# Gathering relation products instead of node rows: a graph network kernel with tables of products, 128 edges a gather, 128 nodes a window

## What is computed

```python
def _rgcn_conv(x, src, dst, et, basis, comp, root, bias):
    W = jnp.einsum('rb,bio->rio', comp, basis)          # 8 matrices 128 x 128
    xw = jnp.einsum('ni,rio->nro', x, W)
    msgs = xw[src, et]
    seg = dst * N_REL + et
    summed = jax.ops.segment_sum(msgs, seg, num_segments=N_NODES * N_REL)
    cnt = jax.ops.segment_sum(jnp.ones((msgs.shape[0],), x.dtype), seg, num_segments=N_NODES * N_REL)
    mean = summed / jnp.maximum(cnt, 1.0)[:, None]
    agg = mean.reshape(N_NODES, N_REL, HIDDEN).sum(axis=1)
    return agg + x @ root + bias
...
for l in range(N_LAYERS):
    h_new = jax.nn.relu(_rgcn_conv(h, src, dst, edge_type, basis[l], comp[l], root[l], bias[l]))
    h = h_new + h
x = _layernorm(x + h, axis=-1)
```

## Time and profile before

| | |
|---|---|
| median of 3 runs | 5051.21 us |
| the profiled execution, its own time | 5047.87 us |
| its span, first to last instruction | 5046.1 us |
| granted TensorE clock, mean | 0.829 of full |
| busy: PE, ACT, DVE, POOL | 65%, 45%, 36%, 76% of the span |
| moved by DMA | 241.73 MB, 48 GB/s |

### The profile page before, as it was taken

The page is one execution under the profiler, slowest core; times in us unless marked ns, Lnnn a source line. Parts: engine busy times, 40 slices in busy tenths (PEclk is TensorE's granted clock), DMA queues, the critical chain, the costliest instruction groups (busy, mean ns, idle before and its releaser), DMA issues.

```text
span 5046.1 us, 91632 instructions
## 1 busy us (share of the span) xinstructions
PE 3255.1 (65%) x20895; PEld 3007.8 (60%) x20895; DVE 1839.1 (36%) x6662; ACT 2286.4 (45%) x6539; POOL 3838.0 (76%) x3447
## 2 busy tenths in 40 slices
PE   6277766666666666666676666666666666666667
PEld 4166665666555566655555656655665665656656
DVE  8444433333333333333333333333333333333335
ACT  4165544444444444444454444444444444444445
POOL 7877777777777777777767777777777777777775
PEclk9599988877888888888888887788778778887888
DMA  6111111111111111111121111111111111111114
GB/s 106 51 41 43 44 43 44 43 43 44 43 44 43 43 44 43 44 43 43 43 80 44 43 44 43 43 44 43 44 43 43 44 43 44 43 43 44 43 44 119
DMA packets 287032, 241.73 MB, mean 48 GB/s; under 512 B 164335, under 2 KB 238267, under 8 KB 286987
## 3 DMA queue, kind: packets, MB, share of 16 engines
q0 software_dynamic: 216448, 209.55, 16.7%
q10 hardware_dynamic: 32488, 15.69, 1.4%
q1 hardware_dynamic: 38051, 15.98, 1.2%
HBM read 224.50 MB, written 14.44 MB: 47 GB/s over the span
## 4 chain that ended last, share of the span: by engine, by line
POOL 55%; issue 42%; DMA 1%; DVE 1%; SPq 0%; PE 0%; ACT 0%; POOLq 0%; DVEq 0%; ACTq 0%
POOL ring L299 54%; POOL S L333 0%; DMA h_rows<-S 0%; DMA S<-counts,idxg 0%; SPq L366 0%; DMA ring<-x,idx 0%; DVE W L267 0%; ACT S L562 0%; PE bank L662 0%; DVE aggT L859 0%; PE bank L673 0%; POOL aggT L348 0%; DVE hT L890 0%; DMA onehot<-x 0%; DVE S L837 0%
## 5 line engine op out<-in xcount | busy, mean ns | idle before, releaser
L662 PE MATMUL bank<-onehot,rows 119*128 119x128 f32 x9856 | 1702.2, 328 | 1618.4 <-ACT rows L523 1456.4
L523 ACT ACTIVATE rows<-ring,relnorm 119x128 f32 x4928 | 1569.0, 389 | 2520.4 <-SPq L401 1755.2
L662 PEld LDWEIGHTS bank<-onehot,rows 119*128 119x128 f32 x9856 | 1476.1, 230 | 1811.1 <-issue 1040.4
L299 POOL DMA_INDIRECT ring<-x,idx x1600 | 1807.8, 1130 | 543.5 <-issue 526.6
L299 POOL DMA_INDIRECT ring<-h_rows,idx x1600 | 1762.5, 1102 | 537.4 <-issue 524.0
L849 DVE TENSOR_TENSOR onehot<-bank,relnorm 119x512 f32<-119x512 f32 x1232 | 851.4, 691 | 1764.5 <-issue 1266.3
L673 PE MATMUL bank<-S,W 128*128 128x128 f32 x9856 | 1488.4, 316 | 1.4 <-ACT S L505 1.4
L673 PEld LDWEIGHTS bank<-S,W 128*128 128x128 f32 x9856 | 1455.7, 234 | 1.8 <-ACT S L505 1.8
L859 DVE TENSOR_TENSOR aggT<-aggT,bank 128x16 f32 x4928 | 833.4, 169 | 1337.1 <-PE bank L673 843.1
L505 ACT ACTIVATE S<-bank 128x512 f32<-128x512 f32 x1232 | 708.0, 575 | 15.1 <-PE bank L662 14.8
L299 POOL DMA_INDIRECT ring<-h_rows,idx_rest x81 | 89.2, 1102 | 26.0 <-issue 26.0
(11 more groups left out here) (114 smaller groups left out, 587.2 us busy)
## 6 DMA issues: line engine op xcount, KB each, us to landing
ring<-x,idx POOLq DMA_INDIRECT x1600
ring<-h_rows,idx POOLq DMA_INDIRECT x1600
S<-x ACTq DMA_DIRECT2D x24, 256.0 KB, 4.0
h_rows<-S SPq DMA_DIRECT2D x24, 256.0 KB, 3.0
onehot<-x ACTq DMA_DIRECT2D x24, 256.0 KB, 3.4
out<-S SPq DMA_DIRECT2D x24, 256.0 KB, 3.2
idx<-srcT SPq DMA_DIRECT2D x64, 23.2 KB
ring<-x,idx_rest POOLq DMA_INDIRECT x81
```

The costliest lines, as they stand in the source:

```text
L299: g.indirect_dma_start(out=ring[0:R, slot * P:(slot + 1) * P], out_offset=None, in_=table, in_offset=bass.IndirectOffsetOnAxis(ap=index, a ...
L523: s.activation(rows[0:R, u % 2 * BATCH + k, :], ring[0:R, bass.ds(v[2 * k + 1], P)], ACT.Copy, scale=relnorm[0:R, 1, bass.ds(b * BATCH + k ...
L662: last = t.matmul(bank[2 * (u % 2) + k // 4][:, k % 4 * P:(k % 4 + 1) * P], rows[0:R, at, :], onehot[0:R, at, :], start=True, stop=True)
```

## The change

At the head of a layer every node is multiplied by all eight W, and the products are stored in a DRAM table of 100,000 rows of 128 numbers (row 8 n + r for node n and relation r), one table a layer. 98 tiles of up to 128 nodes are taken in turn: two matmuls 128 x 512 (`multiply`), two ACT copies into one of six stages of 4 KB per partition (`keep_products`; the stages lie in `ring`), one store of 512 KB from SP's queue (`store_products`). The first gather of the layer waits for all 98 stores. The gathers then fetch product rows by the index 8 src + relation, which DVE makes at the head and which goes through a DRAM tensor `idxT`.

A tile is 128 edges: 1563 tiles. A window is 128 nodes: 98 windows. The 0/1 matrix is 128 edges x 128 nodes and the scatter's result is the sum itself. `S`, its copies (L505) and `project` (L673) are gone. There are 1563 + 98 - 1 = 1660 steps in 208 batches. DVE adds 128 x 128 numbers a step, straight from the scatter's PSUM banks, one batch behind (AFTER = 1). `h1_rows` and its transposes, copies and stores are gone. Layer 0's W are made between the transposes of x, layer 1's after the products of layer 0. The root products follow the table.

```diff
-    R = 119
+    R = 128
...
-    WIN = P // RELS
+    WIN = P
...
-    h1_rows = nc.dram_tensor("h1_rows", (N, H), F32).ap()
+    products = [nc.dram_tensor(f"products{n}", (N * RELS, H), F32).ap() for n in range(LAYERS)]
+    idxT = nc.dram_tensor("idxT", (R, TILES), I32).ap()
...
+        stage = ring[:, 0:STAGES * RELS * H].rearrange("p (s c) -> p s c", s=STAGES)
...
+            pool.wait_ge(idx_made, 1)
+            g.dma_start(idxT, src_all).then_inc(idx_out, 16)
...
+            for L in layers:
+                for q in range(STAGES):
+                    pool.wait_ge(L.stored[q], 16 * stored_count(q))
+                turn(L, 0)
...
+            def store_products(L):
+                for i in range(NODE_TILES):
+                    w = tile_nodes_of(i)
+                    sp.wait_ge(L.staged, 2 * i + 2)
+                    sp.dma_start(products[L.n].rearrange("(n r) f -> n (r f)", r=RELS)[w, :],
+                                 stage[0:w.stop - w.start, i % STAGES, :]).then_inc(L.stored[i % STAGES], 16)
...
+            def keep_products(L):
+
+                for i in range(NODE_TILES):
+                    n = tile_nodes_of(i).stop - i * P
+                    if i >= STAGES:
+                        act.wait_ge(L.stored[i % STAGES], 16 * (i // STAGES))
+                    for half in range(2):
+                        j = 2 * i + half
+                        act.wait_ge(L.multiplied, j + 1)
+                        s.activation(stage[0:n, i % STAGES, half * 512:(half + 1) * 512],
+                                     bank[T_BANKS[L.n][j % len(T_BANKS[L.n])]][0:n, :], ACT.Copy).then_inc(L.staged, 1)
...
-                    if k % 4 == 3 and (not isinstance(b, int) or b >= 1) and not is_last(b):
-                        keep_half(L, b - 1, (u + UNROLL - 1) % UNROLL, k // 4)
...
+            def multiply(L, i):
+
+                w, banks = tile_nodes_of(i), T_BANKS[L.n]
+                for half in range(2):
+                    j = 2 * i + half
+                    if j >= len(banks):
+                        pe.wait_ge(L.staged, j - len(banks) + 1)
+                    t.matmul(bank[banks[j % len(banks)]][0:w.stop - w.start, :], hT[:, w],
+                             W[:, L.n, half * 512:(half + 1) * 512], start=True, stop=True).then_inc(L.multiplied, 1)
...
-            def project(L, b, u, lots):
-
-                pe.wait_ge(L.s_kept, 2 * b + 2)
...
+                if not isinstance(b, int) or b >= PB:
+                    pe.wait_ge(L.added, (b - PB + 1) * BATCH)
...
-                if k == 0:
-                    dve.wait_ge(L.projected, b + 1)
+                if k % 4 == 0:
+                    dve.wait_ge(L.scattered, 2 * b + k // 4 + 1)
...
-            AFTER = 3
+            AFTER = 1
```

More of the change, by code:

```diff
@@ L189, in __init__ @@
                 self.landed = sem(f"landed_{n}")
+                self.multiplied, self.staged = sem(f"multiplied_{n}"), sem(f"staged_{n}")
+                self.stored = [sem(f"stored{k}_{n}") for k in range(STAGES)]
                 self.root_made = sem(f"root_made_{n}")
@@ L237, in by_pool @@
         def by_pool(L, c):
[L239 removed]
+            return L.n == 1 and c % 2 == 1
         def nodes(c):
@@ L493, in _, with start_agg @@
+            def start_agg(L, c):
+                act.wait_ge(L.root_made, c + 1)
+                s.activation(aggT[:, c * CH:c * CH + width(c)], bank[c % 2][:, 0:width(c)], ACT.Identity,
+                             bias=biasT[:, L.n:L.n + 1]).then_inc(L.agg_ready, 1)
+            keep_products(layers[0])
+            for n in range(RELS * BASES, LAYERS * RELS * BASES):
+                scale_diag(n)
+            keep_w(2)
+            keep_w(3)
             for k in range(GROUPS):
-                if k % 2 and FREE + k // 2 < CHUNKS:
-                    start_agg(layers[0], FREE + k // 2)
@@ L498, in _ @@
                              ACT.Copy).then_inc(table_kept, 1)
-            def keep_half(L, b, u, half):
-                act.wait_ge(L.scattered, 2 * b + half + 1)
-                if half == 0 and (not isinstance(b, int) or b >= 2):
-                    act.wait_ge(L.projected, b - 1)
-                s.activation(S[:, u % 2, half * 512:(half + 1) * 512], bank[2 * (u % 2) + half][:], ACT.Copy
-                             ).then_inc(L.s_kept, 1)
+            for c in range(CHUNKS):
+                start_agg(layers[0], c)
             def weigh_batch(L, b, u, late):
@@ L625, in _ @@
             last.then_inc(bounds_from_pe, 1)
-            pe.wait_ge(weights_in, 64)
-            for n in range(W_FIRST):
-                w_product(n)
+            pe.wait_ge(x_kept, CHUNKS)
+            pe.wait_ge(w_kept, 2)
+            L = layers[0]
+            multiply(L, 0)
+            pe.wait_ge(to_pe, 1)
+            t.matmul(carry_psum, before[:], sched[:, 1, P - 1:P], start=True, stop=True).then_inc(from_pe, 1)
+            multiply(L, 1)
             pe.wait_ge(bounds_to_pe, 2)
```

464 lines of the change are left out of this document (211 added, 253 removed).

## The result

The changed kernel takes 4416.17 us (4415.64 to 4417.79, 4 runs), the kernel before 5050.95 us on the same chip (5049.69 to 5052.8, 4 runs): ratio 0.8744, 95% interval 0.8728 to 0.8759. So it is faster, by 12.6% and by the mechanism that was forecast, but 84 us under the forecast and 24 us under the range. (In the rows TensorE is PE, VectorE DVE, ScalarE ACT, GpSimd POOL and SyncE SP.

A forecast was written before the change was run, and what follows sets the result against it. POOL's row of gathers and their issue was taken as the bound. Head 249, gathers 1991, between layers 190, gathers 1991 and tail 72 made 4493 us of span, forecast 4500 us; own range 4440 to 4600, stated range 4440 to 4990.

The forecast's parts named there:

- (a), the work of a gather: Gather loops: 1563 gathers of 128 rows a layer at 0.94 us of work each replace 1681 of 119 at 1.102.
- the rival of 1.512 us: Gather loops: price scales with rows from the large gathers, 1.512 us each, 5234 us in all; chance 0.13.
- the 0.023 for the long gaps: Gather loops: 0.023 us a gather for occasional longer gaps, added to 1.251 to give 1.274 us, 1991 us a layer.
- The lower end of the range: Whole kernel: own range from 4440 us, with table 174 to 200 us twice, head 60 to 75, and drains.
- (b), the table: Head of each layer: PE sets the time of the table products, 174 us, bounds 174 and 200 us.
- (c), between the layers: Last gather of layer 0 to first of layer 1: 190 us, with a 10 us drain and 174 us of products.
- (d), the head: Start of layer 0: 65 us until table products, then 174 us of products; first gather at 249 us.
- (e): Behind POOL: all work fits beside the gathers, DVE 7.2 us of a 9.57 us batch; removed projections worth nothing by themselves.
- a price kept at 1.429 us: Rival in the gather loops: large gathers stay at 1.429 us whatever their rows, 4974 us; chance of this family 0.13.
- work growing with bytes (1.015 us): Halfway rival in the gather loops: work grows with bytes from the small gathers', 4720 us; chance of this family 0.13.
- landings: Rival in the gather loops: rows over 51 MB land slowly; at 9 us a gather costs 1.5 us, 5190 us; chance 0.02.
- VectorE's wide adds: Rival behind the gathers: adds hold up POOL, 5450 us, or come 0.8 us apart, 4925 us; together chance 0.04.

The follow-up runs named there:

- gathers_128: Changed kernel with the sums left out in both layers (ScalarE's weighting, one-hot products, VectorE's additions), 128 edges in a tile: 4405.4 us, one run.
- gathers_124: Changed kernel with the sums left out in both layers and 124 edges in a tile instead of 128: 5784.2 us, one run.
- gathers_126: Changed kernel with the sums left out in both layers and 126 edges in a tile instead of 128: 4574.1 us, one run.
- narrow_128_d: Kernel before with 128 edges in a tile instead of 119, no table, two waits bounded by a maximum with 1, no assertions: 4151.7 us, ratio 0.8210.
- the three jobs with assertions: Sets of runs whose edited kernels had assertions on SyncE's loaded wait numbers; the kernel before took 5773, 5770 and 5948 us in them.

## Why the prediction was right or wrong

- **What bounds the kernel, and that it stays so: right.** The chain is gathers and their issue, and gathers_128, without the sums, has a layer no shorter (1954.4 us for 1951.8).
- **(a), the work of a gather: right.** 0.94 us was taken from the small gathers, not 1.185 scaled up by rows; the runs gave 944 ns, and the rival of 1.512 us is far off. The rule of the Trainium skill that was weighed there pointed the right way, and gathers_124 and gathers_126 bear it out where rows alone would mislead.
- **(a), "and with it the 0.023 for the long gaps": the step that failed.** The small gathers' own cadence, 48.80 / 39 = 1.251 us, was at hand and fell within 0.2% of the 1.2487 us measured. To it was added a term read from gathers of 119 rows. It belongs to those: a long gap every 55 with 119 rows, none steady with 128, in every kernel without assertions. Forty small gathers in a row were too few to show whether they had it. The term made 36 us a layer, 72 in all; another 7 are 1.251 in place of 1.2487. The sum was 77.5 too high. With 1.2487 it gives 249 + 190 + 72 + 3126 x 1.2487 = 4414 us of span. The other 6 us between 4500 and 4416 are the 5 added from span to median, where 1 was needed, and rounding.
- **The lower end of the range failed with it.** 4440 was put down to bounds of table, head and drains, while the gap term had none below it, though no row of 128 indices stood behind it. With the prediction's own lower bound for a gather, 1.251 us, the sum is 4422 us of span, under the range already.
- **(b), the table: right in what bounds it,** TensorE at 0.88 us a product by the earlier trace rows, 0.86 measured. 174 us were forecast for the products and 4.6 for the last store; the timeline has 2216.57 to 2391.08, 174.5 for both. The DMA bound of 182 us, from stores of 512-byte rows at 281 GB/s, was too dear: rows of 4 KB went at 404 GB/s with the engines full.

```profile
2215.83 14.83 DVE L887 SCALAR_TENSOR_TENSOR hT<-aggT,hT 128x512 f32<-128x512 f32 x25
2216.57 23.98 PE L619 MATMUL bank<-W,hT 128*128 128x512 f32 x52 [4.09 <-DVE hT L887]
```

- **(c), between the layers: right,** 184.6 for 190; the drain was 2215.83 - 2206.49 = 9.3 us for 10.
- **(d), the head: right in size, not in its detail.** ScalarE's first copy of x came at 30.97 instead of some 11 us after one load that held ScalarE's queue for 22.75 us, and TensorE's first table product at 71.09 instead of 65; the 184 us from there to the first gather held (183.6).

```profile
5.89 22.75 ACTq L464 DMA_DIRECT2D rows<-comp  x1
...
30.97 1.08 ACT L486 ACTIVATE hT<-bank 128x512 f32<-128x512 f32 x2
```

- **(e): right that all of it hides,** and wide adds took 287 ns as worked out. The batch of 7.2 us was too long: adds, comparisons and what VectorE waited for issue before them are 953.7 + 572.6 + 868.4 us, of which 203 are two single waits outside the loops. The other 2192 us are 5.3 us in each of 416 batches of 9.38 us, 56% and not 75. The removed projections were worth nothing by themselves, which narrow_128_d shows directly: with them a layer 1 takes 1954.7 us.
- **The rivals:** a price kept at 1.429 us or scaled up by rows is refuted by the 944 ns, and work growing with bytes (1.015 us) too; landings stayed at 2.5 us over the 51 MB; VectorE's wide adds didn't hold up GpSimd, whose gathers are as long in gathers_128 (946 ns), where there are none. The rivals' times were added up with 502 us for the rest, where the sum's own terms are 249 + 190 + 72 = 511; that changes none of the chances.

## What to carry to other kernels

Where one instruction issued in a row bounds a kernel, its price is found whole, work and cadence, from instances of the size that it will have; a part of it measured at another size (here the long gaps) is a term of its own, with a lower bound of zero, until a row at the new size shows it. Before a kernel is rebuilt around a better tile size, the size is tried alone: here it took 905 us off, and the rebuild by itself cost 219 us. And a count of gathered rows is chosen for its divisors too: 124 rows in a gather were dearer than 119, and those with a divisor of 15 or 16 (112, 120, 128) were the cheapest in work. Of these only 128 is known to be free of long gaps.

## What the hardware showed that was not expected

- A gather of 124 rows works 1281 ns, one of 119 rows 1080, of 126 rows 973, of 128 rows 946 and of 112 rows 921; GpSimd's queue sends 80, 64, 48, 32 and 32 packets for them, those for the places without rows included. The filled-in packets look like the cost, but no run measured that by itself.
- The long gaps stand at a fixed distance: every 30 gathers with 31 rows in a share, every 55 with 17, every 100 with 9 and every 125 with 7. One more than the rows in a share, times the distance, is 960, 990, 1000 and 1000. By the same count 128 rows, with 8 in a share, would have one about every 110, and they have none in 3124 intervals. Why is open.
- Table stores with 4 KB rows ran at 404 GB/s on one core with the DMA share at 1.02.
- In the three jobs with assertions register instructions of SyncE, ScalarE and VectorE took 0.70 us now and then instead of 40 ns; the kernel before was 14 to 18% longer there and the changed one, with assertions, 22 to 24%.
